# Later steps for ScalarE's side work in a Mamba scan, and a router's small tables in PSUM

## What is computed

```python
dA = jnp.exp(jnp.einsum('bti,is->btis', delta, A))             # 256 channels i, 16 states s
dBu = jnp.einsum('bti,bts->btis', delta * u, B_ssm)
def step(h, inp):
    dA_t, dBu_t, C_t = inp
    h = dA_t * h + dBu_t
    return h, jnp.einsum('bis,bs->bi', h, C_t)
...
y = y + u * D_param
y = y * jax.nn.silu(z)
x = x + (y @ out_proj_w.T + residual)
# router, on the layer-normed x
router_probs = jax.nn.softmax(x_flat @ gate_w, axis=-1)        # 8 experts
expert_idx = jnp.argmax(router_probs, axis=-1)
expert_w = router_probs at expert_idx
```

## Time and profile before

| | us |
|---|---|
| median of 3 runs (lowest, highest) | 1367.31 (1366.61, 1368.74) |
| the profiled execution | 1359.86 |
| its span | 1358.1 |
| scan stage, first to last scan | 158.5 to 595.8 |
| end of the scan stage, router's tail | to 634.8 |
| first expert layer | 635 to 835 |
| attention with the second router | 835 to 1252 |
| second expert layer | from 1252 |

### The profile page before, as it was taken

The page is one execution under the profiler, slowest core; times in us unless marked ns, Lnnn a source line. Parts: engine busy times, 40 slices in busy tenths (PEclk is TensorE's granted clock), DMA queues, the critical chain, the costliest instruction groups (busy, mean ns, idle before and its releaser), DMA issues. The chain is left out here.

```text
span 1358.1 us, 26011 instructions
## 1 busy us (share of the span) xinstructions
PE 1087.7 (80%) x7230; PEld 732.7 (54%) x7230; DVE 957.2 (70%) x2037; ACT 898.7 (66%) x1865; POOL 513.2 (38%) x318
## 2 busy tenths in 40 slices
PE   1776488878788787863895899999999999992697
PEld 1333366666666675651894345454454445541696
DVE  5899577778788788854664467685776768673465
ACT  1787698989889798941673466665766566660564
POOL 0467377677767767861443000101101010111244
PEclk9888699899899899977998799999999999995899
DMA  3000132223254235321332100000000000000321
GB/s 83 2 3 2 32 87 86 74 84 93 78 173 133 91 116 156 90 67 51 95 94 63 47 1 1 17 1 17 13 3 16 1 16 0 16 17 33 97 88 49
DMA packets 50616, 74.26 MB, mean 55 GB/s; under 512 B 7351, under 2 KB 28604, under 8 KB 50528
## 3 DMA queue, kind: packets, MB, share of 16 engines
q1 hardware_dynamic: 41504, 51.09, 13.2%
q0 software_dynamic: 5568, 12.66, 2.6%
q10 hardware_dynamic: 3456, 9.46, 2.3%
HBM read 57.86 MB, written 16.24 MB: 55 GB/s over the span
## 5 line engine op out<-in xcount | busy, mean ns | idle before, releaser
L951 DVE TENSOR_TENSOR_SCAN h<-d_a,p_dbu 128x1024 f32<-128x1024 f32 x128 | 291.0, 2282 | 79.3 <-ACT d_a L738 55.4
L685 POOL TENSOR_TENSOR h<-h,c_rep 128x1024 f32<-128x1024 f32 x128 | 301.5, 2366 | 113.9 <-DMA c_rep<-c_rows 71.1
L1833 ACT ACTIVATE at_probs<-at_scores,at_min 128x512 f32<-128x512 f32 x256 | 183.7, 722 | 136.0 <-DVE at_min L1943 87.0
L1195 POOL DMA_INDIRECT expert_rows<-r_row,r_dest x64 | 62.9, 982 | 503.7 <-DVEq L1121 488.2
L1943 DVE CUSTOM_DVE_ANT_0 at_scores<-at_p_scores,arena 128x512 f32<-128x512 f32 x256 | 174.4, 684 | 89.8 <-PE at_p_scores L1709 50.2
L828 PE MATMUL p_dbu<-ident,b_du_T 128*128 128x128 f32 x1024 | 189.6, 306 | 55.4 <-ACT b_du_T L731 52.9
L731 ACT ACTIVATE b_du_T<-arena,b_T 128x256 f32<-128x256 f32 (+1 forms) x512 | 216.9, 496 | 0.3 <-ACT arena L712 0.2
L828 PEld LDWEIGHTS p_dbu<-ident,b_du_T 128*128 128x128 f32 x1024 | 117.2, 150 | 119.9 <-issue 66.8
L738 ACT ACTIVATE d_a<-arena,a_exp 128x511 f32<-128x511 f32 (+1 forms) x256 | 169.3, 710 | 0.7 <-DVE h L951 0.6
L1716 PE MATMUL at_p_probs_T<-ident,at_probs 128*128 128x128 f32 x1024 | 158.9, 283 | 5.3 <-ACT at_probs L1833 4.6
L1716 PEld LDWEIGHTS at_p_probs_T<-ident,at_probs 128*128 128x128 f32 x1024 | 112.7, 142 | 91.2 <-issue 68.0
(11 more groups left out here) (211 smaller groups left out, 1484.1 us busy)
## 6 DMA issues: line engine op xcount, KB each, us to landing
c_rep<-c_rows SPq DMA_DIRECT2D x128, 256.0 KB, 3.3
f_row<-expert_rows SPq DMA_DIRECT2D x78, 129.0 KB
arena<-in_w_all ACTq DMA_DIRECT2D x8, 578.0 KB, 4.0
arena<-bias_by_distance ACTq DMA_DIRECT2D x8, 448.0 KB, 3.8
x_tok<-in_x SPq DMA_DIRECT2D x4, 512.0 KB, 5.4
x_tok<-x_between SPq DMA_DIRECT2D x8, 256.0 KB, 2.8
expert_rows<-f_pad SPq DMA_DIRECT2D x10, 129.0 KB, 3.1
expert_rows<-f_pad ACTq DMA_DIRECT2D x8, 129.0 KB, 3.1
```

Source lines behind the costliest of these rows:

```text
L685: nc.gpsimd.tensor_tensor(h[:, s % HS, :, :], h[:, s % HS, :, :], cc, ALU.mult).then_inc(prod_done, 1)
L951: nc.vector.tensor_tensor_scan(h[:, s % HS, :, :].rearrange("p c t -> p (c t)"), da[:, s % 2, :, :].rearrange("p c t -> p (c t)"), p_dbu[: ...
L1833: nc.scalar.activation(pr[:, s % 2, :], sc[:, s % 2, :], ACT.Exp, scale=-1.0, bias=mn[:, s % 2:s % 2 + 1]).then_inc(probs_ready, 1)
```

## The change

Four things are edited.

1. On ACT all copies of turned tiles now stand behind a `scale`, and at later steps: `turn_g` at steps 6 and 7 (before: both at 6), `turn_du` at 9 and 10 (before: both at 8), `act_rows` at 13 and `act_turned` at 14 (before: both at 12), `act_rstd` at 11 (before: 10), and the router's exponentials two batches back at step 1 (before: one batch back at step 15).
2. PE, DVE and POOL follow: `turn_g` on PE behind steps 5 and 6, `project` 7, `next_du` 8 and 9, `pe_turn` 13, `pe_logits` 14, `pe_ranks` 2. The router's DVE stages 0 to 5 stand at steps 8, 9, 9, 11, 14, 15, and stages 6 to 11 at steps 0 to 5 of the next batch. `pool_send` stands at step 7 instead of 5.
3. In the first router the tables `logit`, `pos`, `idx` and `slot` lie in PSUM. The logits are read where PE leaves them, without a copy; the other three lie in the second half of `p_small`'s bank. LN's epsilon is given to ACT as a bias, so the instruction that added it on DVE goes.
4. In both routers the addition of 512 to the token numbers (L1118) goes from DVE to POOL, ahead of the four sends, with a wait for its own end.

```diff
-    DVE_STEPS = 24
+        self.in_psum = scratch is not None
+        if self.in_psum:
+            n = TPB * E_N
+            self.pos = scratch[:, 0:n].rearrange("p (j e) -> p j e", j=TPB)
+            self.idx, self.slot = scratch[:, n:n + TPB], scratch[:, n + TPB:n + 2 * TPB]
+            self.logit, self.eps = p_small[:, 0:n].rearrange("p (j e) -> p j e", j=TPB), sb("eps", [P, 1])
+            self.steps = 21
...
-            EARLY = {0: 7, 1: 8, 2: 8, 3: 10, 4: 12, 5: 13, 6: 14, 7: 15}
-            LATE = {8: 0, 9: 2, 10: 3, 11: 3}
+            EARLY = {0: 8, 1: 9, 2: 9, 3: 11, 4: 14, 5: 15}
+            LATE = {6: 0, 7: 1, 8: 2, 9: 3, 10: 4, 11: 5}
...
-            self._step(V.tensor_copy(self.logit[:], small(0)))
+            if not self.in_psum:
+                self._step(V.tensor_copy(self.logit, small(0)))
...
-            self._step(ts(self.row[:, :, ID_AT], self.row[:, :, ID_AT], float(T), None, ALU.add))
...
-        self.k.nc.scalar.activation(self.lnv[:], self.veps, ACT.Ln).then_inc(self.act_step, 1)
+        self.k.nc.scalar.activation(self.lnv[:], self.mv[:, :, 1], ACT.Ln, bias=self.eps[:]).then_inc(self.act_step, 1)
...
     def pool_send(self, pool, b):
         pool.wait_ge(self.rows_ready, 1 + b)
         pool.wait_ge(self.row_filled, 1 + b)
         self.k.passed(pool)
+        ids = self.row[:, :, ID_AT]
+        self.k.nc.gpsimd.tensor_scalar(ids, ids, float(T), None, ALU.add).then_inc(self.ids_next, 1)
+        pool.wait_ge(self.ids_next, 1 + b)
+        self.k.passed(pool)
         for j in range(TPB):
             self.k.nc.gpsimd.indirect_dma_start(
```

More of the change, by code:

```diff
@@ L688, in batch @@
                 for s in range(NS):
-                    if s == 5 and not (isinstance(b, int) and b < 2):
+                    if s == 7 and not (isinstance(b, int) and b < 2):
                         rt.pool_send(pool, b - 2)
@@ L741, in early, with late, batch @@
             def early(b, s, after_scale):
-                if s == 6:
-                    turn_g(b, int(after_scale))
-                elif s == 10 and not after_scale:
+                if s in (6, 7) and after_scale:
+                    turn_g(b, s - 6)
+                elif s == 11 and not after_scale:
                     rt.act_rstd(act, b)
-                elif s == 12 and not after_scale:
+                elif s == 13 and after_scale:
+                    rt.act_rows(act, b)
+                elif s == 14 and after_scale:
                     rt.act_turned(act, b)
-                elif s == 12:
-                    rt.act_rows(act, b)
-                elif s == 15 and not after_scale:
+            def late(b, s):
+                if s == 1:
                     rt.act_exps(act, b)
-            def batch(b, first=False, last=False, load=None):
+            def batch(b, number, last=False, load=None):
                 for s in range(NS):
-                    for after_scale in (False, True):
-                        if after_scale:
-                            scale(b, s)
-                        if not first:
-                            early(b - 1, s, after_scale)
-                        if s == 8 and not last:
-                            turn_du(b + 1, int(after_scale), p_x)
+                    if number > 0:
+                        early(b - 1, s, False)
+                    scale(b, s)
+                    if number > 0:
+                        early(b - 1, s, True)
+                    if number > 1:
+                        late(b - 2, s)
+                    if s in (9, 10) and not last:
+                        turn_du(b + 1, s - 9, p_x)
                     exps(b, s)
@@ L887, in batch @@
                 for s in range(NS):
-                    if number > 0:
-                        early(b - 1, s, False)
-                    if s == 8 and not last:
-                        next_du(b + 1, 1)
                     spread(b, s)
@@ L918, in _ @@
                 late(B - 2, s)
-                for after in (False, True):
-                    if (s, after) in ((11, False), (12, False)):
-                        n = (s - 11) * 4
-                        at.flip(pe, n, n + 4)
-                    early(B - 1, s, after)
+                if s in (13, 14):
+                    n = (s - 13) * 4
+                    at.flip(pe, n, n + 4)
+                early(B - 1, s)
             at.flip(pe, 8, 12)
-            late(B - 1, 1)
+            late(B - 1, 2)
             at.flip(pe, 12, 2 * H)
@@ L1045, in _wait @@
     def _wait(self, dve, b):
-        dve.wait_ge(self.dve_step, 1 + b * self.DVE_STEPS + self.at)
+        dve.wait_ge(self.dve_step, 1 + b * self.steps + self.at)
     def start_dve(self, dve):
```

112 lines of the change are left out of this document (62 added, 50 removed).

## The result

The changed kernel takes 1349.86 us (median of 4 runs, 1346.49 to 1353.69), the kernel before, beside it on the same chip, 1368.03 (1366.61 to 1370.01): a ratio of 0.9876, 95% interval 0.9853 to 0.9898. The forecast was 1347.5 in a range of 1341 to 1358. The profiled execution took 1349.78, its span is 1347.9.

The account below looks back on a forecast made before the run. Once ACT's waits go, POOL with C's DMA bounds the scan: 384 + 23.4 (sends) + 7.0 + 2 + 2.4 = 418.8 us against 438.3. With -0.6 and +0.3 outside, 1367.3 - 19.8 = 1347.5; range 1341 to 1358.

Parts of the forecast that it names:

- ACT's waits go, and POOL with C is what is late next: Scan: all 46.6 us of ACT's waits before five lines go; POOL with C's DMA then sets 3.0 us a step.
- 128 products at 3.0 us, and the excess of two batches: POOL in the scan: 384 us, plus 7.0 for late C in two batches with large loads on ACT's DMA queue.
- 2 us of waits for scans: POOL in the scan: 2 us waiting for DVE's scans, in batch 1 when the normed rows (L1078) stretch.
- 0.4 us for the addition on POOL, bounds 0.2 to 1.2: POOL in the scan: each token-number addition with its wait takes 0.4 us; six make 2.4, bounds 1 to 7.
- Sum for the scan: First product to last end: 414.4 + 2 + 2.4 = 418.8 us against 438.3, so 19.5 less.
- The tail 0.6 less, the second router 0.3 more: Behind the last product and in the second router: 0.6 us less and 0.3 more, bounds together -1.5 to +2.
- The tables in PSUM are worth nothing on the end by themselves, only as cover: Router on DVE: stretches vanish, hidden by slack; without this cover DVE late by up to 2.3 us a batch, once.
- The offset of 7.4 us: Whole kernel: median of runs lies 7.4 us above the profiled execution; kept for the changed kernel, 1340.1 becoming 1347.5.
- Signs: Changed profile: scan waits under 10 us, C waits over 80, stretch near 419, clock at least 0.94, DVE awaits sums.
- ACT's pace: Rival, 5%: in the scan ACT alone sets the pace, gaining all 46.6 us of its waits, 1320.7.
- The new wait for landed rows: Rival, 22% for its kind: normed rows wait for the later send; six batches lose about 2 us each, 1359.5.
- The slower clock: Rival, 5%: PE waiting for POOL in the scan lowers TensorE's clock; 25 steps at the lower level give 1380.

Follow-up runs that it names:

- second pair of profiles: Kernel before and changed kernel, both unchanged, profiled once more: spans 1359.8 and 1344.7 us; the changed kernel's stretch 422.9, ratio 0.985.
- first series of experiments: On one chip: both kernels unchanged (medians 1364.62 before, 1345.83 changed), parts 1 and 2 alone (1353.04), parts 3 and 4 alone (1361.39).

## Why the prediction was right, and where not

The mechanism was right: POOL with C's DMA sets the pace once ACT waits less. The time, 1349.86 in place of 1347.5, was right in part by luck. The sum foresaw 19.8 us less, but the profiled execution became only 10.1 faster (1359.86 to 1349.78). The medians moved by 18.2, because the timed runs of the kernel before lie above its profiled one, and those of the changed kernel don't. Inside the sum for the scan one term was too large and two were too small: 418.8 was forecast, and 424.0 and 422.9 were measured.

- *ACT's waits go, and POOL with C is what is late next.* Held. With the old steps four buffers of C bring no gain; with the new ones they take all of POOL's waits for C away and shorten the stretch by 9 to 16 us (ratio 0.9764 against 0.9801 and 0.985). The five waits went from 46.6 to 9.0 us (under 10 was forecast). But ACT's waits were not "gone": 17.9 us stand before the copy of the rows, which I had passed over. I had reckoned one more step and a `scale`, 4.5 us, as cover for the wait of 2.4 behind the normed rows; with the copy of the rows ahead of `act_turned`, and with the normed rows slower, this wait grew from 17.1 to 22.0 us in all.
- *128 products at 3.0 us, and the excess of two batches.* The forecast has 414.4 less six sends of 5.2 each, 383.2, for products and C. They took 301.3 + 74.9 = 376.2. The term was 7.0 too large, and the wait for C was not over 80. Part of it is no error of pace: where POOL waits for a scan, C lands meanwhile.
- *2 us of waits for scans.* They were 11.3, so the term was 9.3 too small. The place was right: nine of the eleven waits after the first product, 8.9 us, lie ahead of the first send. The longest is 2.93, in batch 1, behind four stretched normed rows. I had priced this one event and none of the others. In the second profile of the changed kernel the waits are 6.4.
- *0.4 us for the addition on POOL, bounds 0.2 to 1.2.* This is the step that failed. It takes 0.23 + 0.88 = 1.1 where it stands, near the upper bound. The sends took 36.5 in place of 31.2 + 2.4, so 2.9 more, and taking the addition off that place gave 6 to 11 us, against some 18 for the whole change. I took the value from the nearest row by size, a cast of 0.19 us. The dear part was an indirect DMA that comes to its wait too early, and for this the trace of before has rows, though with DVE as the engine waited for: 0.87 to 0.90 us, 37 times in the first expert layer.
- *Sum for the scan.* -7.0 + 9.3 + 2.9 = 5.2 us more than forecast, so 14.3 saved in place of 19.5.
- *The tail 0.6 less, the second router 0.3 more.* The tail became 1.0 longer, in the second pair of profiles 1.2 (35.6 to 36.8), so the sign was wrong; over all kernels it lies between 35.0 and 36.8, and why is not shown. The part from the first expert layer to the second grew by 2.7 us (617.4 to 620.1, in the second profiles 616.5 to 618.2). With the addition on DVE in both routers it is 616.6 in one kernel and 619.0 in another; with the addition ahead of the second router's sends it lies between 616.9 and 620.2. So a price of the addition there is not shown. The three misses, 5.2 in the scan, 1.6 in the tail and 2.4 here, make 9.2 of the 9.7 us by which the profiled execution missed the sum.
- *The tables in PSUM are worth nothing on the end by themselves, only as cover.* Alone it nearly held (0.9974). As cover the tables were priced too low: I had set up to 2.3 us a batch, once; with the steps alone ACT waits 24.8 us for the epsilon instruction in seven batches, 3.5 each. A router instruction on PSUM stays at 0.2 us (L1111, 178 ns), as forecast. A small one on SBUF can last to the end of POOL's product (2.37 us from 272.83, with four buffers). The Trainium skill, "SBUF — State Buffer", section on the engine ports, describes a lock between DVE and GpSimd held for the whole instruction, and the trace agrees; the 3.02 us from 297.76 show besides that DVE need not get in between two products that stand back to back. What I had missed is that when POOL waits less, its products stand back to back or start with the end of a scan, and both are bad places for a small DVE instruction.
- *The offset of 7.4 us.* It does not carry over to the changed kernel: there the profiled execution (1349.78) lies at the median. By the medians of the first series of experiments the change is worth 18.8 us (1364.62 to 1345.83), between the two pairs of profiled spans 10.2 and 15.1 us. The kernel before scatters by 13 us from run to run, the changed one by 5 and 7. So of the 18 us that the medians show, the profiles explain 10 to 15; where the kernel before spends the rest in its longer runs stays open. One hint: no kernel with the tables in PSUM scatters by more than 8 us (parts 3 and 4 alone: 5, over 12 runs, in the series in which the kernel before had 13), while the new steps with the tables in SBUF have 23 over 8 runs; with the tables in SBUF and four buffers of C, where the two engines meet in every batch, it is 4. That fits chance meetings of DVE and POOL, but no long run was profiled, so it is not shown. The forecast of 1347.5 stood on this offset: from the profiled execution alone it was 1340.1, and 1349.78 was measured.
- *Signs.* DVE's waits did not move from `d_a` to PE's sums: 44.9 for `d_a` and 11.4 for the sums. POOL's waits for scans were to be under 10 us and a sign of being wrong above 15; without the one before the first product they were 11.3. The stretch was to be near 419 and was 424.0. The granted clock in the scan was 0.93, just under the 0.94 named.
- *Rivals.* ACT's pace (1320.7) needed C off the path; with four buffers and the addition off POOL the kernel comes to 1325.87. The new wait for landed rows is there (5.3 us on L1093) and costs nothing that a run can tell: the ratio is 0.983 without it and 0.985 with it. The slower clock did not come.

## What to carry to other kernels

When side work is moved, look at the engine whose waits shrink and ask what it will now run beside: here small DVE instructions on SBUF cost up to 1 us on average while POOL starved, and three of them 2 to 3 us each when it didn't. So take them off SBUF, or off the meeting point, before feeding POOL better. When two instructions wait for the same thing, the first of them has the wait: add up the waits of both before calling one of them gone. Put an instruction whose end an indirect DMA must wait for ahead of a long one on the same engine, not between the long one and the DMA. To price an instruction in a new place, look in the whole trace for its wait, not only for its size. And take the base of a forecast from more than one profiled run and three timed ones.

## What the hardware showed that was not expected

- An indirect DMA of POOL starts 0.15 to 0.18 us after a product when its own waits are long fulfilled, but 0.87 to 0.90 us after the end of an instruction that it has to wait for, whether that is a small one of POOL or one of DVE. A product behind the small POOL instruction, which has nothing to wait for, starts after 0.16.
- More buffers made the kernel before slower by 2.25%: three small DVE instructions of 128x4 and 128x32 rose to means of 3.09, 2.06 and 1.99 us. The longest lasted in every batch until the product ended behind which POOL had no scan left, in six of seven over the end of a product before it.
- The same kernel on one core took 1358.33 to 1371.39 us in 12 runs of one series, and the kernel with parts 3 and 4 alone, in the same series, 1357.88 to 1362.91 in 12 runs.
